# Graph convolutions on one core: node rows picked with 13 matmuls instead of 14, and the scan's flags in PSUM

## What is computed

```python
def rgcn_conv(x, src, dst, edge_type, W, root, bias):
    x_src = x[src]
    for r in range(8):
        msg = msg + where((edge_type == r)[:, None], x_src @ W[r], 0)
    agg = segment_sum(msg * norm[:, None], dst)
    return agg + x @ root + bias

def _nnconv(x, src, dst, edge_attr, ew, eb, rw, rb):
    W = (edge_attr @ ew + eb).reshape(E, 16, 16)
    msg = einsum('ei,eio->eo', x[src], W)
    return segment_sum(msg, dst) + x @ rw + rb
```

## Time and profile before

| what | us |
|---|---|
| median of 3 runs | 13827.26 (13812.48 to 13847.12) |
| profiled execution, span from first to last instruction | 11719.3 |
| convolutions r0, r1 (first to last pick) | 1053, 963 |
| convolutions c0, c1, c2 | 984, 985, 982 |

### The profile page before, as it was taken

The page is one execution under the profiler, slowest core; times in us unless marked ns, Lnnn a source line. Parts: engine busy times, 40 slices in busy tenths (PEclk is TensorE's granted clock), DMA queues, the critical chain, the costliest instruction groups (busy, mean ns, idle before and its releaser), DMA issues. The chain is left out here.

```text
span 11719.3 us, 162611 instructions
## 1 busy us (share of the span) xinstructions
PE 9568.5 (82%) x41815; PEld 6646.5 (57%) x41815; DVE 9376.0 (80%) x15091; ACT 8305.5 (71%) x16370; POOL 7775.8 (66%) x6242
## 2 busy tenths in 40 slices
PE   6888888888887149996998488888899969978996
PEld 2333333333333037775776377777677757766775
DVE  8999999999998777874555599999577757766775
ACT  5777777777776127775887388888488758866884
POOL 4555555555556538886777777776377767776776
PEclk7666666666666579998999799999799989989998
DMA  3444444444444347775886111111589868977895
GB/s 129 179 176 177 178 176 179 176 179 174 180 174 157 134 152 274 275 269 190 268 265 218 44 44 44 44 45 37 163 306 307 276 215 307 308 243 250 306 307 174
DMA packets 750673, 2256.03 MB, mean 193 GB/s; under 512 B 272727, under 2 KB 420974, under 8 KB 674126
## 3 DMA queue, kind: packets, MB, share of 16 engines
q10 hardware_dynamic: 161280, 1027.68, 24.6%
q1 hardware_dynamic: 388638, 984.49, 22.4%
q0 software_dynamic: 200624, 242.28, 9.2%
HBM read 1321.88 MB, written 931.97 MB: 192 GB/s over the span
## 5 line engine op out<-in xcount | busy, mean ns | idle before, releaser
L589 POOL DMA_INDIRECT h<-in_x,idx x1568 | 2090.3, 1333 | 1628.9 <-DMA efT<-in_edge_attr_t 1192.3
L673 ACT ACTIVATE PX<-PX,h 128x16 f32<-128x16 f32 x12544 | 2509.6, 293 | 6.4
L622 PE MATMUL PS<-M,minus_ident 128*128 128x512 f32 x1568 | 1419.3, 1031 | 308.6 <-DVE M L707 308.6
L1950 POOL DMA_INDIRECT myg<-node_table,mix x784 | 1199.3, 1530 | 385.9 <-issue 249.1
L1983 PE MATMUL PS<-mhr,lhs 128*128 128x392 f32 x6272 | 1249.5, 354 | 245.1 <-DVE lhs L2152 244.6
L1449 PEld LDWEIGHTS PS<-every_weight,dstf 112*128 112x128 f32 x8960 | 1225.6, 192 | 226.6 <-DVE dstf L1581 117.0
L2048 ACT ACTIVATE mhr<-mhb 128x1568 fp32r<-128x1568 bf16 x784 | 1141.5, 1504 | 293.3 <-DVE mhb L2141 285.9
L1449 PE MATMUL PS<-every_weight,dstf 112*128 112x144 f32 (+1 forms) x8960 | 1259.7, 284 | 96.9 <-DVE dstf L1581 96.4
L1983 PEld LDWEIGHTS PS<-mhr,lhs 128*128 128x128 f32 x6272 | 1133.5, 191 | 337.5 <-ACT mhr L2048 273.8
L610 PE MATMUL PS<-waug,efT 17*128 17x256 f32 x6272 | 1042.8, 534 | 320.1 <-DVE e L685 290.6
L610 PEld LDWEIGHTS PS<-waug,efT 17*128 17x128 f32 x6272 | 612.8, 251 | 1052.4 <-issue 483.9
(11 more groups left out here) (418 smaller groups left out, 20490.0 us busy)
## 6 DMA issues: line engine op xcount, KB each, us to landing
softmax_maxima<-M SPq DMA_DIRECT2D x196, 1024.0 KB, 3.9
softmax_denominators<-ST SPq DMA_DIRECT2D x196, 1024.0 KB
softmax_numerators<-ST SPq DMA_DIRECT2D x196, 1024.0 KB
one_hot_rows_of_sources<-r0hb ACTq DMA_DIRECT2D x224, 896.0 KB
r1hb<-one_hot_rows_of_sources ACTq DMA_DIRECT2D x224, 896.0 KB
c0hb<-one_hot_rows_of_sources ACTq DMA_DIRECT2D x224, 896.0 KB
c1hb<-one_hot_rows_of_sources ACTq DMA_DIRECT2D x224, 896.0 KB
c2hb<-one_hot_rows_of_sources ACTq DMA_DIRECT2D x224, 896.0 KB
```

The source lines that it names most:

```text
L589: PO.indirect_dma_start(h[b.k][:, at(q), :], None, io["x"], bass.IndirectOffsetOnAxis(ap=idx[b.k][:, q:q + 1], axis=0))\
L622: mm = PE.matmul(PS[0:CH, 4 + n, :], minus[:, :], M[b.k % 2][:, n::4, :], start=False, stop=True)
L673: act = S.activation(PX[b.k][:, 1, t, D * i:D * i + D], PX[b.k][:, 0, t, D * i:D * i + D], ACT.Copy, scale=h[b.k][:, t, i:i + 1])
L1950: PO.indirect_dma_start(yg[b.k][:, q, :], None, table8, bass.IndirectOffsetOnAxis(ap=ix[b.k][:, q:q + 1], axis=0)).then_inc(m_g[b.k], 16)
```

## The change

Nodes are numbered anew: A8 = 8 groups of KB = 6 slices of 128 nodes (6144), and the last 106 nodes as a slice of their own, `last_parts`, whose high and low part stand side by side in 32 columns. So a group is picked with 2 x 6 matmuls of 128 columns and one of 32, on the third slot of the seventh place (`LOWEST = 6`). In the sum, features of the last nodes' high part land on partitions 0 to 15 and of their low part on 16 to 31. An edge of the last nodes therefore must keep group 0 on partitions 0 to 15 and group 1 on the others: two tables of groups, `pick_group` and `pick_group_of_low_parts`, are made in the setup in place of one, and `ra` is loaded with two DMAs, 16 and 112 partitions. `mask` and `weigh_rows` go over 128 partitions instead of 112. The scan's flags `kp` stand in PSUM banks 2 and 3, one buffer instead of two in SBUF; `keeps` waits for the scan of the block before instead of the one before that.

```diff
-A9, KT = 7, 7
+A8, KB, KT = 8, 6, 7
+ROWS = 128 * KB
...
-            for n, d_ in enumerate((pick_a, pick_b)):
+            for n, d_ in enumerate((pick_a, pick_low, pick_b)):
...
-            V.tensor_scalar(pab[0][:, :], pab[1][:, :], float(128 * KT), None, ALU.is_ge).then_inc(*vd.up())
-            for k in range(2, A9):
+            V.tensor_scalar(pab[0][:, :], pab[2][:, :], float(ROWS), None, ALU.is_ge).then_inc(*vd.up())
+            V.tensor_scalar(pab[1][:, :], pab[2][:, :], float(A8 * ROWS), None, ALU.is_ge).then_inc(*vd.up())
+            for k in range(2, A8):
...
+            V.scalar_tensor_tensor(out=pab[0][:, :], in0=pab[1][:, :], scalar=-float(A8 - 1), in1=pab[0][:, :],
+                                   op0=ALU.mult, op1=ALU.add).then_inc(*vd.up())
+            V.wait_ge(*vd.now())
+            V.tensor_tensor(pab[1][:, :], pab[0][:, :], pab[1][:, :], ALU.add).then_inc(*v2t.up())
...
             for k in range(NT):
-                for n in TWO:
+                for n in range(3):
+                    if 3 * k + n in (0, 32):
+                        V.wait_ge(t2v.sem, turned_of + min(3 * k + n + 32, 3 * NT))
                     V.tensor_copy(pT[0:wd[k], k, n, 0:CH], spread_at(k, n)).then_inc(*pT_up.up())
...
-        parts = sb("parts", [128, 2, KT, A9 * D], F32R)
+        parts = sb("parts", [128, 2, KB, A8 * D], F32R)
+        last_parts = sb("parts_of_last_rows", [128, 2 * D], F32R)
...
-                    kp.append(sb(f"{name}kp{k}", [CH, D, TBC], F32, L))
+                    kp.append(PS[0:CH, 2:4, :].rearrange("p b c -> p (b c)")[:, 0:D * TBC].rearrange("p (f t) -> p f t", f=D))
...
-            mx = [dstf[0:A9 * D, 512 * k:512 * k + 512] for k in range(1 + LAG)]
+            mx = [dstf[:, 512 * k:512 * k + 512] for k in range(1 + LAG)]
...
-                SP.dma_start(ra[half][:, :], rows(b, half, pick_a)).then_inc(h_ra[half].sem, 16)
+                SP.dma_start(ra[half][0:D, :], rows(b, half, pick_a, D)).then_inc(h_ra[half].sem, 16)
+                SP.dma_start(ra[half][D:128, :], rows(b, half, pick_low, 128 - D)).then_inc(h_ra[half].sem, 16)
...
                     for m in range(m0, m1):
-                        mm = PE.matmul(PS[0:A9 * D, 4 + q % 2, :], parts[:, m % 2, m // 2, :],
-                                       hot_[q % 2][:, m // 2, :], start=(m == 0), stop=(m == 2 * KT - 1))
+                        if m == LOWEST:
+                            PE.matmul(PS[0:2 * D, 4 + q % 2, :], last_parts[:, :], hot_[q % 2][:, KB, :], start=False, stop=False)
+                            continue
+                        n = m - (m > LOWEST)
+                        mm = PE.matmul(PS[:, 4 + q % 2, :], parts[:, n % 2, n // 2, :],
+                                       hot_[q % 2][:, n // 2, :], start=(m == 0), stop=(m == PICKS - 1))
...
                 def keeps(b):
-                    if due(n := b.on(-2).count(1, 1)):
+                    if due(n := b.on(-1).count(1, 1)):
                         S.wait_ge(*c_run.at(n))
```

More of the change, by code:

```diff
@@ L217, in program @@
         si = sb("srci", [CH, T], I32, setup)
-        pab = [sb(f"pab{k}", [CH, T], F32, setup) for k in TWO]
+        pab = [sb(f"pab{k}", [CH, T], F32, setup) for k in range(3)]
         NT = (T + 127) // 128
-        pT = sb("pT", [128, NT, 2, 128], I16, setup)
+        pT = sb("pT", [128, NT, 3, 128], I16, setup)
         wd = [min(128, T - 128 * k) for k in range(NT)]
@@ L370, in setup_vector @@
             V.wait_ge(*src_in.next(16))
[L371 removed]
+            V.tensor_copy(pab[2][:, :], si[:, :]).then_inc(*vd.up())
             V.wait_ge(*vd.now())
[L373 to L374 removed]
+            V.tensor_scalar(pab[0][:, :], pab[2][:, :], float(ROWS), None, ALU.is_ge).then_inc(*vd.up())
+            V.tensor_scalar(pab[1][:, :], pab[2][:, :], float(A8 * ROWS), None, ALU.is_ge).then_inc(*vd.up())
+            for k in range(2, A8):
                 V.wait_ge(*vd.now())
[L376 removed]
+                V.scalar_tensor_tensor(out=pab[0][:, :], in0=pab[2][:, :], scalar=float(k * ROWS),
                                        in1=pab[0][:, :], op0=ALU.is_ge, op1=ALU.add).then_inc(*vd.up())
             V.wait_ge(*vd.now())
[L379 to L380 removed]
+            V.scalar_tensor_tensor(out=pab[2][:, :], in0=pab[0][:, :], scalar=-float(ROWS), in1=pab[2][:, :],
+                                   op0=ALU.mult, op1=ALU.add).then_inc(*vd.up())
+            V.wait_ge(*vd.now())
+            V.scalar_tensor_tensor(out=pab[0][:, :], in0=pab[1][:, :], scalar=-float(A8 - 1), in1=pab[0][:, :],
+                                   op0=ALU.mult, op1=ALU.add).then_inc(*vd.up())
+            V.wait_ge(*vd.now())
+            V.tensor_tensor(pab[1][:, :], pab[0][:, :], pab[1][:, :], ALU.add).then_inc(*v2t.up())
             V.wait_ge(*pT_up.now())
[L382 removed]
+            turned_of = t2v.taken
             for k in range(NT):
[L384 removed]
+                for n in range(3):
+                    if 3 * k + n in (0, 32):
+                        V.wait_ge(t2v.sem, turned_of + min(3 * k + n + 32, 3 * NT))
                     V.tensor_copy(pT[0:wd[k], k, n, 0:CH], spread_at(k, n)).then_inc(*pT_up.up())
+            t2v.next(3 * NT)
             V.wait_ge(*vd.now())
@@ L395, in setup_tensor @@
             for k in range(NT):
-                for n in TWO:
+                for n in range(3):
+                    if 3 * k + n == 32:
+                        PE.wait_ge(pT_up.sem, 1 + 32)
                     PE.transpose(spread_at(k, n), pab[n][:, 128 * k:128 * k + wd[k]], ident[0:CH, 0:CH])\
                         .then_inc(*t2v.up())
-            PE.wait_ge(*pT_up.next(2 * NT + 1))
+            PE.wait_ge(*pT_up.next(3 * NT + 1))
         setup_sync()
@@ L1293, in program @@
         LOOP = dict(n=NBC, tb=TBC)
+        PICKS = 2 * KB + 1
+        LOWEST = 6
         def conv(no, name, edge, weights, always=None):
@@ L1356, in weighed, with rows @@
                 return PS[:, bank:bank + 2, :].rearrange("p g (t c) -> p (g t) c", c=256)
-            def rows(b, half, from_):
-                return from_[some(b, NG + 16 * half, 16), :].rearrange("(a t) c -> a (t c)", a=1).to_broadcast([128, 2048])
+            def rows(b, half, from_, n=128):
+                return from_[some(b, NG + 16 * half, 16), :].rearrange("(a t) c -> a (t c)", a=1).to_broadcast([n, 2048])
             def load_low(b, half):
@@ L1449, in weigh_rows @@
                         mm = PE.matmul(weighed(q)[:, r, 0:R * D], mx[q % (1 + LAG)][:, 128 * r:128 * r + 128],
-                                       every[0:A9 * D, 0:R, :].rearrange("p r o -> p (r o)"))
+                                       every[:, 0:R, :].rearrange("p r o -> p (r o)"))
                     mm.then_inc(h_sel.sem, 1)
                 def steps(nx, b):
-                    at = 2 * KT if both else 9
+                    at = PICKS if both else 9
                     for q in range(HG):
@@ L1798, in whole @@
                     of.base += 16 * NBC // 2
-                for of in h_ra + make * h_rb:
+                for of in h_ra:
+                    of.base += 32 * NBC
+                for of in make * h_rb:
                     of.base += 16 * NBC
```

35 lines of the change are left out of this document (21 added, 14 removed).

## The result

The changed kernel took **14440.7 us** (14425.6 to 14466.7, four runs) beside 13820.3 us for the kernel before on the same chip: a ratio of **1.044 (1.041 to 1.046), 620 us slower**. The forecast was 13625 us and faster, its range ended at 13850. It was wrong in sign.

A forecast was written before the change was run, and what follows sets the result against it. PE and POOL were taken to bound it within 4% of each other, POOL last. Gains 126 (c0 to c2) + 62 (r1) + 28 (r0) - 14 (setup) = 202 us; 13827 - 202 = 13625 us, range 13540 to 13850.

The forecast's parts named there:

- the sum: Whole kernel: 202 us saved, taken one for one from the 13827 us median, with 2108 us above the span constant.
- r1: Convolution r1: block falls from 34.4 to PE's 32.1 us, POOL's 31.8 below it; gain 62 us, bounds 27 and 87.
- c0 to c2: Three convolutions: the scan no longer stretches 27 gathers by 1.56 us; gain 42 us each, 126 in all.
- The 32-column matmul costs one pitch: Pick groups: the narrow matmul takes 0.231 us like the others, so groups shorten to 3.91 us (r1) and 4.00 (c).
- The rival of the draining array: Pick groups: the 32-column matmul changes the tile and PE drains, 0.2 to 0.28 us per change, two a group; chance 0.37.
- Flags in PSUM spare the gather: Gather beside the scan: falls to 0.94 us, saving all 1.56 us in c, while the scan keeps its 2.02 us.
- POOL 33.7 stays above PE's 33.0: Block of c0 to c2, in us: POOL 35.2 - 1.5 = 33.7 still sets the time; PE 32.0 + 1.0 = 33.0.
- PE binds everywhere: Rival, all convolutions: every gather stretch shrinks as in r1, c gains 62 us each, r0 70, total 13523 us; chance 0.05.
- Only the scan's share: Convolution r0: only the scan's stretch of 26 gathers by 1.05 us goes; gain 27, rounded to 28 us, bounds 0 and 70.
- Setup: Before the convolutions: more passes, transposes, copies and stores that nothing hides; 13.4 us longer, taken as 14.

The follow-up runs named there:

- The picks alone: Changed kernel's 13 pick matmuls, but scan flags in two SBUF buffers; against the kernel before: smooth 11381.7 us (0.970), paused 14340.3 us (1.056).
- the flags only: Kernel before (14 pick matmuls of 112 columns) with the scan's flags in PSUM, one buffer: smooth 11575.1 us (0.987), paused 13824.5 us (1.018).
- the 14th matmul: Changed kernel plus a matmul of 32 zero columns in each group, back to the old pace: paused 14685.7 us beside 13924.4 for before (1.053).

## Why the prediction was wrong

**The step that failed** is in the sum: "the median is 2108 us above it; I take that part as constant and the saving one for one". A gap of 18% between a profiled span and the times was taken as something outside the program. No run shows such a part outside the span: the span was of the smooth condition, the times of the paused one. What differs lies inside, as pauses of TensorE in the very stages that were changed. The kernel before in the paused condition (span 13541.9 us) is 1822 us longer than in the smooth one, 311 of them in r1, 484, 491 and 473 in c0 to c2, and 14 in r0. A part that large, with no row for it, couldn't be held constant: the changed kernel has more of it. No rival of mine was about it.

By stages, all paused, first mask to last, changed less before: r0 1435 - 1058 = +377, r1 1547 - 1268 = +279, c0 to c2 +61, +54 and +69, the edge stage between r1 and c0 +46, up to r0 +27. (The two traces are from comparisons whose before differ by 2%, so these sum to 911 us, and not to 620.)

**In the condition that the prediction read, its steps can be checked one by one**, 11719 us against the changed kernel's smooth 11288:

- *The 32-column matmul costs one pitch*: right. Its load takes 0.11 us, its matmul follows 0.23 us behind the one before, and padding it changed nothing. In c1, smooth:

```profile
9656.58 0.11 PEld L1464 LDWEIGHTS PS<-c1hot,parts_of_last_rows 128*32 128x32 f32 x1
9656.81 0.39 PE L1464 MATMUL PS<-c1hot,parts_of_last_rows 128*32 128x512 f32 x1
9656.81 1.35 PEld L1467 LDWEIGHTS PS<-c1hot,parts 128*128 128x128 f32 x6
9657.04 1.57 PE L1467 MATMUL PS<-c1hot,parts 128*128 128x512 f32 x6
```

  The rival of the draining array falls. Groups come every 3.9 us (r1) and 4.0 us (c), as forecast. The Trainium skill (TensorEngine Tiling (Array Packing), Key Properties) says that a change of the tiling mode drains TensorE. Here the change from a tile of 128 x 128 to one of 128 x 32 and back cost one pitch of 0.23 us, no drain, and the measurement decides.
- *Flags in PSUM spare the gather*: right. Against the earlier trace rows:

```profile
9648.45 2.02 DVE L1719 TENSOR_TENSOR_SCAN c1run<-PS,c1run 128x896 f32<-128x896 f32 x1
9649.04 0.94 POOL L1451 DMA_INDIRECT c1yg<-node_table,c1ix  x1 [0.30 <-issue]
```

  The scan keeps its 2.02 us and the gather 0.94. The Trainium skill (SBUF — State Buffer, Who interferes with whom) says that a DVE instruction with two SBUF inputs contends with a GpSimd instruction that reads SBUF, and one with at most one SBUF input does not. The trace agrees: 27 of the 28 scans of c1 stretched a gather before, none does now.
- *r1*: 65 us gained where 62 were forecast.
- *c0 to c2*: 82 to 83 us each where 42 were forecast. The step "POOL 33.7 stays above PE's 33.0" failed on both sides. PE's block is 32.2 us, so `turn` and `keeps` cost 0.2 and not 1.0; and the gathers' mean fell from 1165 to 1030 ns, 3.2 us a block, of which the scan is 1.5. The picks alone shortened them too, to 1076 ns, and brought the median block to 32.2 us though 26 of 28 scans still stretched a gather. So the stretches shrank with PE's rhythm in c as in r1. POOL is as full as before (692 us busy and 204 of "issue" in 903), but DVE's wait for the gathers, 108 us in the earlier trace rows, is gone: a full POOL was no proof that POOL sets the time. This was the rival "PE binds everywhere", with 62 us each.
- *r0*: 126 us where 28 were forecast. "Only the scan's share" failed the same way: the picks alone bring r0 from 1044 to 939 us, first mask to last. The gathers' mean falls from 1270 to 1069 ns.
- *Setup*: 15 us longer (the first matmul of the first layer starts at 91.6 us in place of 76.5), forecast 14. The first mask of r0 comes 19 us later.

So the smooth condition gains 435 us where 202 were forecast. The sign is right, and so is the mechanism of the matmul, of the flags and of r1; in c and r0, which make up 374 of it, the stretches of the gathers were wrongly held fixed.

## What to carry to other kernels

When a profiled span and the measured times differ by more than their scatter, find out whether both are of one condition before anything is added to one or the other; here the difference was 18%, and the loss lay in it. Where a condition makes TensorE stand still for 15 to 20 us in each block, savings in the block's groups don't show, and a stage that newly gets the stretch costs more than they bring: compare stage by stage, in both conditions, before a change of TensorE's work is called a gain. Two engines within 4% of each other aren't to be priced one after the other, since stretches that depend on their overlap shrink when the rhythm changes.

## What the runs showed of the hardware that was not expected

- In the paused condition TensorE starts its instructions 0.7 to 2.8 us apart for 15 to 20 us (pitch otherwise 0.23 us), or sends its signals 14 us late, while gathers and DVE's operations keep their lengths. It begins at a granted clock of 1.0; the clock goes to 0.5 during it and stays there for some 20 us, once in each block of some 55 us.
- In this condition the length of the group doesn't order the kernels: c1 takes 1476 us in the kernel before (groups of 4.2 us), 1507 with the picks only (4.0), 1532 in the changed kernel (4.0), 1532 with the flags only (4.2) and 1559 with the 14th matmul (4.2). The flags in PSUM, a gain of 1.3% otherwise, cost 1.8% here; by which way isn't known.
- By the clock records of c1, the stretches at a granted clock of 1.0 that are longer than 20 us last 27 to 38 us each, apart from the stage's first, in the kernel before and in the changed one alike; in the smooth condition the changed kernel has one of 901 us. With some 20 us at 0.5 behind each, that makes the block of 52.6 and 54.9 us. It fits that the rhythm of the pauses, and not the group, sets c's block, but no run shows it.
- A scan with one operand in PSUM takes 2.02 us, as with both in SBUF, and leaves a gather beside it at 0.94 us in place of 2.57. With both in SBUF, the stretched gather ended 0.75 us behind the scan, in all 27 cases of c1.
